# Megakernel of a macaron layer on one core: weight issues moved and spread, shared tiles at both ends of the last segment, norm and router placed inside products, the overflow table split from the ranks

## The reference

```python
x = x + 0.5 * ffn(layernorm(x))     # 8 experts, top 2, and 2 shared ones
x = x + ssm(layernorm(x))           # selective scan over 256 steps
x = x + 0.5 * ffn(layernorm(x))     # same weights as the first
```

```python
# ffn, for token rows t
scores = sigmoid(x @ w_router.T)
topk_w, topk_i = top_k(scores, 2); topk_w /= topk_w.sum()
out = sum over both chosen e: topk_w * ((silu(x @ wg[e].T) * (x @ wu[e].T)) @ wd[e].T)
out += sum over j in 0, 1: (silu(x @ sg[j].T) * (x @ su[j].T)) @ sd[j].T
# ssm, per channel d with 16 states n
dt, B, C = softplus(xp[:256]), xp[256:272], xp[272:]     # xp = x @ W_xproj.T
h = exp(dt * A) * h + dt * B * x;  y = sum_n h * C + D * x
```

## Time and profile before

| what | value |
|---|---|
| three runs | 531.19, 531.88, 533.93 us; median 531.88 |
| the profiled execution | 529.17 us, span 527.2 us |
| mean granted TensorE clock | 0.998 |
| busy: PE, DVE, ACT, POOL | 508.2, 324.4, 158.6, 231.4 us |
| HBM read and written | 48.89 and 18.22 MB |

### The profile page before, as it was taken

The page is one execution under the profiler, slowest core; times in us unless marked ns, Lnnn a source line. Parts: engine busy times, 40 slices in busy tenths (PEclk is TensorE's granted clock), DMA queues, the critical chain, the costliest instruction groups (busy, mean ns, idle before and its releaser), DMA issues.

```text
span 527.2 us, 11153 instructions
## 1 busy us (share of the span) xinstructions
PE 508.2 (96%) x4410; PEld 414.2 (79%) x4411; DVE 324.4 (62%) x658; ACT 158.6 (30%) x337; POOL 231.4 (44%) x208
## 2 busy tenths in 40 slices
PE   8999988989999999999998999999999999999994
PEld 6989975448988999546897799974489999974684
DVE  3742423721665999997679489999966732521224
ACT  1111122222037444545211644445521111212210
POOL 1050100140512999998335289999930352000022
PEclk9999999999999999999999999999999999999999
DMA  7956994860305455551221444555300132210012
GB/s 236 388 225 250 402 396 170 262 219 22 98 14 135 111 117 154 139 144 52 68 84 63 99 127 131 130 155 139 90 22 3 40 111 61 73 47 23 21 52 80
DMA packets 42230, 67.88 MB, mean 129 GB/s; under 512 B 5152, under 2 KB 24992, under 8 KB 42176
## 3 DMA queue, kind: packets, MB, share of 16 engines
q1 hardware_dynamic: 29424, 38.94, 26.0%
q10 hardware_dynamic: 9088, 18.09, 9.2%
q0 software_dynamic: 3664, 10.10, 5.9%
HBM read 48.89 MB, written 18.22 MB: 127 GB/s over the span
## 4 chain that ended last, share of the span: by engine, by line
PE 77%; DVE 8%; DMA 7%; issue 3%; POOL 2%; ACTq 1%; ACT 1%; another core or an unknown queue 1%; POOLq 0%; SPq 0%; DVEq 0%
PE ps L515 33%; PE ps L540 16%; PE ps L530 14%; PE ps L553 7%; DMA w_gu<-in_wu 3%; PE ps L559 2%; PE ps L564 2%; ACTq L810 1%; DMA region<-yg_rows,ypos 1%; DVE xres L1187 1%; PE ps L703 1%; DMA bcb<-bc_rows 1%; DVE hb L1027 1%; POOL region L971 1%; DMA xres<-in_x 1%
## 5 line engine op out<-in xcount | busy, mean ns | idle before, releaser
L515 PEld LDWEIGHTS ps<-xt,w_gu 128*128 128x128 f32 x1400 | 161.6, 192 | 9.4 <-issue 6.4
L515 PE MATMUL ps<-xt,w_gu 128*128 128x128 f32 x1400 | 164.2, 276 | 3.6 <-ACT xt L794 2.4
L1027 DVE SCALAR_TENSOR_TENSOR hb<-hb,ps 128x640 f32<-128x640 f32 x68 | 55.5, 816 | 123.2 <-ACT hb L776 113.8
L540 PE MATMUL ps<-w_dn,hb 128*128 128x256 f32 x520 | 120.7, 379 | 0.0
L540 PEld LDWEIGHTS ps<-w_dn,hb 128*128 128x128 f32 x520 | 94.8, 190 | 10.8
L776 ACT ACTIVATE hb<-ps 128x640 f32<-128x640 f32 x68 | 47.6, 700 | 180.7 <-PE ps L515 152.0
L1072 DVE TENSOR_TENSOR_SCAN ps<-ps,region 128x512 f32<-128x512 f32 x64 | 78.3, 1223 | 8.0 <-ACT ps L867 4.9
L515 PE MATMUL ps<-xnt,w_gu 128*128 128x128 f32 x680 | 80.8, 276 | 2.1 <-DVE xres L1042 2.0
L1005 POOL TENSOR_TENSOR xnt<-xnt,hh 128x512 f32<-128x512 f32 x64 | 81.7, 1278 | 2.5 <-DVE hh L1077 2.5
L515 PEld LDWEIGHTS ps<-xnt,w_gu 128*128 128x128 f32 x680 | 78.8, 192 | 4.5 <-DVE xres L1042 2.4
L530 PE MATMUL ps<-w_gu,xt 128*32 128x512 f32 (+2 forms) x768 | 74.6, 524 | 3.0 <-issue 3.0
(11 more groups left out here) (112 smaller groups left out, 320.7 us busy)
## 6 DMA issues: line engine op xcount, KB each, us to landing
bcb<-bc_rows SPq DMA_DIRECT2D x22, 512.0 KB, 5.1
region<-bc_rows SPq DMA_DIRECT2D x10, 512.0 KB, 5.1
xg<-xg_rows SPq DMA_DIRECT2D x35, 128.0 KB
w_gu<-in_wg ACTq DMA_DIRECT2D x7, 640.0 KB, 12.1
w_gu<-in_wu ACTq DMA_DIRECT2D x7, 640.0 KB, 13.3
w_dn<-in_wd ACTq DMA_DIRECT2D x7, 640.0 KB, 14.6
yg_rows<-ob SPq DMA_DIRECT2D x20, 128.0 KB, 3.5
xg_rows<-bcb SPq DMA_DIRECT2D x1, 2176.0 KB, 14.7
```

The lines of the kernel that those rows point to most:

```text
L515: last = nc.tensor.matmul(gup(p)[:, c * P:(c + 1) * P], w_gu4[:, e, k, c * P:(c + 1) * P], x, start=(k == 0), stop=(k == KC - 1))
L540: ins = nc.tensor.matmul(outp(p), hb[:, p, c * P:(c + 1) * P], w_dn4[:, e, c, :], start=(c == 0), stop=(c == IC - 1))
L1027: nc.vector.scalar_tensor_tensor(out=h, in0=h, scalar=1.0, in1=gup(p)[:, 0:I], op0=ALU.add, op1=ALU.mult).then_inc(s_a, 1)
```

## The change

It has five parts.
1. `LATE` is split: expert 1 is issued by ScalarE in `first(3)`, ahead of the copy of tile 5's rows, expert 2 behind tile 3 as before. Expert 6 moves from behind tile 5 into `first(6)`, behind tile 7's tanh.
2. In segment 3 one shared tile moves from ahead of the routed ones behind them: four at each end.
3. The four operations of the table are a step of their own, "table", and stand later than the ranks. Whoever reads the table waits for `s_pos`.
4. Norm, turn, router and ranks of segment 1 come one tile sooner.
5. For segments 2 and 3 a step "normed" puts the turn of the norm between the first and second piece of a first product, and the router's product behind its last piece. "logits" turns the logits between two tiles, and "ranked behind" puts the two rank products behind a whole first product. The combining of segment 1 is split in two.

```diff
@@ ORDERS
-          SHARED[0] + SHARED[1][:1] + ROUTED + SHARED[1][1:]]
+          SHARED[0] + ROUTED + SHARED[1]]
@@ SCHEDULE
-    ("second", 0), ("tiles", 1, 6), ("N1", "P", 1), ("N2", "P", 1), ("tiles", 6, 8), ("T", "P", 1), ("tiles", 8, 9), ("R1", 1),
+    ("second", 0), ("table", 0), ("tiles", 1, 5), ("N1", "P", 1), ("N2", "P", 1), ("tiles", 5, 7), ("T", "P", 1),
...
-    ("O", 1), ("G", 1), ("first", S1 + 14), ("T", "P", 2), ("second", S1 + 14), ("R1", 2),
-    ("scored", S1 + 15, 2), ("second", S1 + 15), ("ranked", S2 - 1, 2), ("S", 2, 0), ("second", S2 - 1), ("C", 1, 0, TT), ("N1", "A", 1),
+    ("O", 1), ("G", 1), ("normed", S1 + 14, 2), ("second", S1 + 14), ("logits", 2),
+    ("ranked behind", S1 + 15, 2), ("second", S1 + 15), ("C", 1, 0, 2), ("S", 2, 0), ("tiles", S2 - 1, S2),
+    ("C", 1, 2, TT), ("N1", "A", 1), ("S", 2, 1), ("tiles", S2, S2 + 1), ("N2", "A", 1), ("table", 2),
@@ weights
-        LATE = {3: (1, 2), 4: (3, 4), 5: (5, 6), 6: (7,)}
+        LATE = {3: (2,), 4: (3, 4), 5: (5,), 6: (7,)}
+        LATE_MID = {3: (1,), 6: (6,)}
@@ TensorE
             def free_expert(s, group):
+                pe.wait_ge(s_pos, s + 1)
@@ TensorE, first
                 if ranks is not None:
                     rank(ranks)
+                if norm is not None:
+                    turn_norm(("P", norm))
...
                 rest_of_gate_up(n + 1)
+                if norm is not None:
+                    score(norm)
+                if ranks_behind is not None:
+                    rank(ranks_behind)
@@ ScalarE, first
                     tanh(n + 1)
+                for e in LATE_MID.get(n, ()):
+                    send_weights(e)
@@ VectorE, route_rows
                 nc.vector.tensor_copy(ypos[:, s, 1, :], m2[:, :])
+
+            def overflow_table(s):
                 link(nc.vector.tensor_tensor(
                     over, slots[:, :].rearrange("p (j a) -> p j a", a=1).to_broadcast([P, GROUPS_MAX, E]),
                     over_t(cum[:, :], GROUPS_MAX), ALU.is_ge))
@@ VectorE, steps
+                elif kind == "normed":
+                    first(step[1])
+                    copy_logits(step[2])
+                elif kind == "logits":
+                    route_scores(step[1])
```

More of the change, by code:

```diff
@@ L614, in turn_logits, with turn_norm, first @@
                 held[:] = [(s_neg, s + 1)]
-            def first(n, router=None, ranks=None):
+            def turn_norm(which):
+                k = NORM[which]
+                banks_free()
+                for t in range(TT):
+                    pe.wait_ge(s_xn, TT * k + t + 1)
+                    for d in range(KC):
+                        at = (t // 2 * 4 + d * 2 + t % 2) * P
+                        last = nc.tensor.transpose(both_banks[:, at:at + P],
+                                                   xn[which[0]][:, t, d * P:(d + 1) * P], ident[:, :])
+                    if t % 2 == 1:
+                        last.then_inc(s_xnp, 1)
+                held[:] = [(s_xnt, 2 * (k + 1))]
+            def first(n, router=None, ranks=None, norm=None, ranks_behind=None):
                 q = n % 2
@@ L757, in _ @@
                     first(step[1], ranks=step[2])
+                elif kind == "R2":
+                    rank(step[1])
+                elif kind == "normed":
+                    first(step[1], norm=step[2])
+                elif kind == "logits":
+                    turn_logits(step[1])
+                elif kind == "ranked behind":
+                    first(step[1], ranks_behind=step[2])
                 elif kind == "second":
@@ L771, in link, with send_weights @@
                 act.wait_ge(s_ach, chain[0])
+            def send_weights(e):
+                for k, (dst, src) in enumerate(weights_of(e)):
+                    act.dma_start(dst, src).then_inc(s_w[e][k], 16)
             def tanh(n):
@@ L872, in exponentials, with copy_norm @@
                 nc.scalar.activation(ex[:, :, :], ex[:, :, :], ACT.Exp).then_inc(s_ex, 1)
+            def copy_norm(which):
+                for b in range(2):
+                    act.wait_ge(s_xnp, 2 * NORM[which] + b + 1)
+                    ins = nc.scalar.activation(xnt[:, :, b * 2 * P:(b + 1) * 2 * P],
+                                               state_banks[:, b, :].rearrange("p (d t) -> p d t", d=KC), ACT.Copy)
+                    ins.then_inc(s_xnt, 1)
             nc.scalar.preload_act_table_set("exp_and_others")
@@ L877, in _ @@
                 if kind == "T":
[L878 to L882 removed]
+                    copy_norm(step[1:])
                 elif kind == "start":
@@ L1220, in _ @@
                     copy_logits(step[1])
+                elif kind == "R2":
+                    route_rows(step[1])
+                elif kind == "table":
+                    overflow_table(step[1])
                 elif kind == "decay":
```

45 lines of the change are left out of this document (18 added, 27 removed).

## The result

| | before | changed |
|---|---|---|
| median of 7 runs each, side by side | 531.88 us | 537.36 us (535.74 to 539.31) |
| ratio | | 1.0124, 95% [1.0097, 1.0150] |
| the same pair measured again (25 and 6 runs) | 529.94 us | 537.74 us, ratio 1.0153 [1.0124, 1.0182] |
| profiled execution, span | 529.17, 527.2 us | 537.29, 535.5 us |
| mean granted clock of TensorE | 0.998 | 0.990 |

The change costs 1.2 to 1.5%, 5.5 to 7.8 us. The forecast was 531.8 us with 528.8 to 534.5 around it: the sign is wrong and the time lies outside.

The account below looks back on a forecast made before the run. The prediction took TensorE's own instruction order as the bound, busy 508.2 of 527.2 us. Terms -2.1 + 1.3 + 4.2 - 3.5 = -0.1 gave a median of 531.8 us, range 528.8 to 534.5.

Parts of the forecast that it names:

- Weights and the table of segment 0: Up to the first mixed product: earlier weight issues and the table behind tile 1's hidden save 2.1 us.
- its end should move with its beginning: Weight queue: never empty, so starting 2.1 us sooner, its last `wu` lands at 82.8 instead of 84.90.
- The lower bound of 1.0: Weights: least gain, 1.0 us, if only the reorder counts because other transfers fill the start.
- Norm turned inside a product: Halves of segments 2 and 3: 24 of 40 matmuls no longer cover the norm turn, +2.7 us each.
- Ranks behind a product: Halves of segments 2 and 3: TensorE waits 1.4 us for the eviction behind the ranks, +1.5 us each with restart.
- The half of segment 2: Half at 253: losses of 4.2 us less 2.9 us of existing waits that go, +1.3 us.
- The 2.9 of waits (evictions behind ranks and the first combining) go: Half at 253: 39.9 us taken against 37.0 of work; these waits vanish with combining split and ranks moved.
- The late VectorE: Rival, chance 0.1: VectorE starts the scores late, +1.4 us once (533.2 us) or +2.7 in both halves (534.5).
- so the wait of 2.40 at 68.7 left it at full: TensorE's clock: mean 0.998 is used up by the last 2.4 us, so that earlier wait brought no half clock.
- The rival's chance of 0.07: Clock rival: three long TensorE waits each bring half clock, 2.2 us lost each, +6.6 us, 538.4 us; chance 0.07.
- The end: Last half: four shared tiles last bring stores, gathers and combining one tile sooner, the last eviction at 520.8, -3.5 us.
- holds with little to spare: Start of the routed tiles: rows wanted one tile sooner, but positions come 1.4 us sooner and TensorE 4 later.

Follow-up runs that it names:

- woven_only: Kernel before with part 5 alone, its combining split and the table apart in segments 2 and 3: 539.36 us, ratio 1.0187.
- ranks_behind: Changed kernel with the norm turned behind the whole first product, the ranks still behind the next one: 526.57 us, ratio 0.9982 to the kernel before.
- filled_short: Changed kernel with unused products in each half, 5 ahead of the norm turn and 3 ahead of the eviction wait: 533.46 us, ratio 1.0072 to before.
- changed_again: The changed kernel measured once more, nothing altered, on the chip of the later fills: 537.74 us, ratio 1.0153 to the kernel before.
- tail_only: Kernel before with segment 3's tile order alone changed, four shared tiles at both ends: 534.98 us, ratio 1.0097.
- unwoven: Changed kernel with the halves of segments 2 and 3 as before, the table still apart: 532.05 us, ratio 1.0034 to the kernel before.
- norm_in: Changed kernel with the norm still turned inside the first product, but router and ranks as before: 534.42 us, ratio 1.0149 to the kernel before.
- first and third batch: Two groups of follow-up runs, each on a chip of its own; the kernel before took 530.29 us in the first, 529.94 us in the third.
- filled: Changed kernel with unused products in each half, 10 ahead of the norm turn and 6 ahead of the eviction wait: 539.4 us, ratio 1.0165 to before.
- tail_filled_short: Kernel before with only segment 3's tile order changed, plus 9 unused products in the wait for the routed rows: 531.72 us, ratio 1.0041.
- seg3_behind: Changed kernel with segment 2's half as before (table apart); in segment 3 norm turned behind the whole product, ranks behind the next: 526.97 us, 0.9943 of before.
- second and fourth batch: Two groups of follow-up runs, each on a chip of its own; the kernel before took 526.97 us in the second, 527.07 us in the fourth.

## Why the prediction was wrong

The terms add up to +8.3 us in the profiled execution, for a forecast of -0.1. Of the 8.4 us between them 3.9 are half clock, 1.7 a late signal, 1.1 weights that landed later than worked out, 0.9 waits that the kernel before doesn't have, 0.7 the end and 0.1 the half of segment 3.

**Weights and the table of segment 0** (-2.1; found -1.0, and 0.5 to 1.8 in the other kernels with this order). The step "its end should move with its beginning" failed. The first issue came 1.9 sooner, nearly the 2.1 that were worked out, but the windows show 101 GB/s until 44 and 326 in the next 2 us, so that the transfers were 1.3 us ahead and not 1.9. The statement that the row copy "isn't missed" held. TensorE did wait 1.18 us there, but for the load of tile 5's rows: the last scatter ahead of that load is issued at 39.25, before at 38.15, and it didn't come sooner with TensorE. The wait had no consequence. The lower bound of 1.0 was the right value in this pair. One execution of each says little here: kernels with the old order of issues have their first mixed product at 85.57 to 89.03, those with the new order and the table apart at 84.34 to 85.59.

**Norm turned inside a product** (+2.7 in each half). The mechanism was right: waits of 2.22 and 2.22 us, and a turn that takes 0.3 longer (1.15 from start to next start, for 0.87), beside VectorE's four operations of the norm, which end at about the same time.

**Ranks behind a product** (+1.5, of which a wait of 1.4). Right: 1.33 in segment 3, 1.42 in woven_only, 1.33 twice in ranks_behind. Together the half of segment 3 came out at +4.3 for a forecast of +4.2.

**The half of segment 2** (+1.3; found +7.8) is where the forecast broke, in three places.
1. "The 2.9 of waits (evictions behind ranks and the first combining) go": they were 1.8. The 2.9 was a difference of two sums; TensorE's own timeline of before has two waits in that stretch, 0.74 and 1.06, and reading them would have settled it. woven_only shows +2.2, an error of 0.9.

```profile
280.49 1.16 PE L515 MATMUL ps<-xnt,w_gu 128*128 128x128 f32 x8 [0.74 <-DVE xres L1042]
...
288.65 1.16 PE L515 MATMUL ps<-xt,w_gu 128*128 128x128 f32 x8 [1.06 <-DVE xres L1042]
```

2. The late VectorE, which stood as a rival at 0.1 (and is a late signal of TensorE, as shown above), happened at the ranks of both profiled executions of the changed kernel: 1.88 and 2.05 us idle, where woven_only and filled_short have none. It made the wait 3.1 to 3.2 instead of 1.4, about +1.7.
3. The clock, +3.9 in that execution: 1.6 between norm turn and router (5.55 against 3.92 in woven_only), 3.0 behind the second wait (as against changed_again), less 0.7. That much woven_only, at full clock, loses ahead of and at the ranks (0.46 of it a wait for VectorE), while the slower TensorE doesn't.

Over many runs the same shows: of 7.5 us (means of 537.5 and 530.0) 3.2 are the difference in what half clock took, and somewhat more if half clock behind the last product is left out. The 4.2 that stay are close to the sum of the terms found without it: -1.0 + 2.2 + 1.7 + 4.3 - 2.8 = 4.4.

The failed step is the sentence "so the wait of 2.40 at 68.7 left it at full", and with it a price of zero for the clock. One execution in which a wait did no harm was taken as proof for waits of that length. tail_only has nearly the same wait, 2.36 at 66.94, with half clock behind it from 69.98 on. In the 17 profiled executions of this study TensorE waited 30 times for 2.0 to 4.5 us behind its first 20 us. Half clock began within or behind 14 of the 27 waits under 3.5 us (4 of the 8 of 2.2 us ahead of a norm turn), and all three over 4 us. Between those first 20 us and the last product it came nowhere else. So a wait of that length has a price in about every second execution, and the change adds three of them in its halves (2.2, 3.1 and 2.2).

The rival's chance of 0.07 was far too low; its time, 538.4, was near the one measured by luck: it had three falls of 2.2 us each, and two came, of 1.6 and 3.0, beside a late signal. The Trainium skill (TensorE: Matmul & The Clock Gate, Part 1: The HAM clock gate), cited there, says that the gate closes again after idling. The traces agree on that, with 17 of these 30 waits. The use made of it was wrong: in the halves this change doesn't gather short waits into one, it makes new ones.

**The end** (-3.5; found -2.8). The last eviction now follows the last product by 0.5 instead of 4.0 us, -3.5 as worked out from the earlier trace rows, with the combining beside the product. Behind it the output's last store took 3.3 us from issue to landing instead of 2.5. Over the 17 profiles it is 3.3 or 3.4 in nine and 2.3 to 2.5 in eight, always alike for one kernel; why, no run shows. But the sentence that the routed rows' margin "holds with little to spare" was truer than its author acted on. It held only with the rank products moved: in tail_only, unwoven and norm_in, where they stand as before, TensorE waits 4.3 to 4.5 us, which eats the gain of the end. norm_in has TensorE later by the norm's turn and waits all the same, so that delay alone isn't what keeps the margin. Weaving and shared tiles at both ends were thus two parts that pay for each other, and ranks_behind has the cheap half of the weaving that suffices.

**What stays open.** Why signals of TensorE come up to 2.2 us late between 262 and 275 us. It isn't one kernel's doing. They delay VectorE in 8 of the 10 profiles of the first pair and of the first and third batch: at the ranks in the changed kernel twice and in filled (1.85 to 2.05 us idle), at the scores in before, unwoven, tail_only, tail_filled_short and seg3_behind (2.67 to 2.77 us idle). In none of the 7 of the second and fourth batch do they: 1.85 or less at the scores. So it goes with the chip. Where that half is as in the kernel before, it takes 43.05 to 43.18 us with the late signal and 42.04 to 42.05 without. What makes a signal late, no run isolated. Also open is what share of the clock's price is real at each place: changed_again shows 3.0 us for the longer fall, and filled_short supports up to 4.0 of 4.3 us in the halves, but its profile is also one of the two of those ten without the late signal. Ahead of the weights a fill took half clock away without a gain.

## What to carry to other kernels

Work placed between a producer on another engine and its consumer on TensorE is cover: before moving it, count the waits in TensorE's own timeline of the stretch, not as a difference of sums. Price a new TensorE wait of 2 us or more at its length plus half clock behind it in about every second execution, here 1.6 to 3.0 us each in the halves. When several parts are changed together, ask of each whether it stands alone: two orders here share the best place (0.994 and 0.995 of before). One drops parts 2 and 5 whole. The other keeps part 2 and, of the most elaborate part, only the ranks' place in segment 3, which hides the wait for the routed rows.

## What the hardware showed that was not expected

- Half clock behind waits of 2.2 us and more, for 3.4 or 6.8 us, with TensorE busy for all or most of it, and not in each execution of the same program: in changed_again the wait of 3.2 us at 276 left full clock, in the first profile of the same kernel the one of 3.1 did not. That half took 47.96 and 50.93 us.
- A semaphore signal of a matmul can come 2 us after the modelled end of the matmul, while TensorE's next matmuls run (272.08 for 270.29), in the profiles of some chips and not of others.
- Runs of one kernel differ by it: the kernel before took 525.2 us at a mean granted clock of 0.999 and 529.3 at 0.990, on one chip.
- Adding 2.3 and 1.5 us of useless products to each half made the kernel 4.3 us faster, since they stand in waits.
- A weight queue started 1.9 us sooner was only 1.2 us sooner at its end, and 1.1 sooner gave 0.8.
